# V read back once a pass in four transfers of all 128 rows, and the projected rows' transfers issued behind the products, in a three-layer block on one Trainium2 core

## What is computed

```python
q = jnp.einsum('btc,hdc->bhtd', x, Wq); k = jnp.einsum('btc,hdc->bhtd', x, Wk)
gate_v = jnp.einsum('btc,hec->bthe', x, Ws)
w, sel = jax.lax.top_k(gate_v, K)                       # 2 of 8 experts for each head
mix_v = jnp.einsum('bthk,bthke->bthe', jax.nn.sigmoid(w), one_hot(sel))
proj_v = jnp.einsum('btc,edc->bted', x, Wv)             # 8 experts' projections
v = jnp.einsum('bthe,bted->bhtd', mix_v, proj_v)        # V: 16 heads
attn = softmax(q * scale @ k) @ v
res = jnp.einsum('bthe,bthd,efd->bthf', mask_o, attn, Wo)
```

## Time and profile before

| | us |
|---|---|
| median of 3 runs | 2421.73 |
| lowest and highest run | 2420.21, 2424.61 |
| profiled execution, whole | 2416.01 |
| its span from first to last instruction | 2414.2 |
| PE busy | 2316.1 |
| DVE busy | 2032.5 |
| ACT busy | 2020.9 |
| POOL busy | 1157.8 |

### The profile page before, as it was taken

How to read it: one execution, slowest core, us unless ns; L and a number is a source line. 1 busy time by engine, 2 the same in 40 slices (tenths; PEclk the granted TensorE clock), 3 DMA queues, 4 the chain that set the end, 5 groups by cost and what they waited for, 6 DMA issues and landing times.

```text
span 2414.2 us, 120555 instructions
## 1 busy us (share of the span) xinstructions
PE 2316.1 (96%) x49920; PEld 2149.1 (89%) x49920; DVE 2032.5 (84%) x3626; ACT 2020.9 (84%) x6245; POOL 1157.8 (48%) x1126
## 2 busy tenths in 40 slices
PE   3999999999999999999999999999999999999997
PEld 3988888989899999999989999999999999999987
DVE  5888878888888888888888888888888888888874
ACT  3988787888888888888888888888888888888885
POOL 3454545455354454454454454554554554544431
PEclk9999999999999999999999999999999999999999
DMA  4555455655556556556556556555556555555563
GB/s 125 165 162 155 142 153 146 167 159 166 164 156 178 164 158 177 160 156 175 162 163 173 160 161 172 160 162 162 175 157 168 167 163 163 164 164 163 167 171 105
DMA packets 660701, 388.23 MB, mean 161 GB/s; under 512 B 232512, under 2 KB 585664, under 8 KB 660160
## 3 DMA queue, kind: packets, MB, share of 16 engines
q1 hardware_dynamic: 659728, 379.67, 54.9%
q10 hardware_dynamic: 432, 0.85, 0.1%
HBM read 191.64 MB, written 188.74 MB: 158 GB/s over the span
## 4 chain that ended last, share of the span: by engine, by line
PE 83%; ACT 6%; DVE 6%; issue 3%; POOL 1%; DMA 0%; SPq 0%; DVEq 0%; ACTq 0%; POOLq 0%
PE psT L471 18%; PE psS L426 15%; PE psT L488 7%; PE psS L514 7%; PE psT L439 6%; PE psT L514 6%; PE psT L490 6%; PE psT L489 5%; ACT PB L785 5%; PE psT L483 5%; PE psT L453 4%; DVE NMAX L665 2%; DVE QK L729 1%; PE psT L520 1%; PE psT L572 1%
## 5 line engine op out<-in xcount | busy, mean ns | idle before, releaser
L785 ACT ACTIVATE PB<-psS,NMAX 128x256 f32<-128x256 f32 x2048 | 947.3, 497 | 100.8 <-DVE NMAX L665 99.9
L471 PE MATMUL psT<-V,PT 128*64 128x64 f32 x16384 | 541.3, 224 | 9.9 <-issue 9.4
L471 PEld LDWEIGHTS psT<-V,PT 128*64 128x64 f32 x16384 | 503.2, 138 | 37.8 <-issue 12.4
L785 ACT ACTIVATION_READ_ACCUMULATOR PB<-psS,NMAX 128x1 f32 x2048 | 471.2, 230 | 0.0
L426 PE MATMUL psS<-QK 64*128 64x256 f32 x6144 | 464.0, 290 | 1.2 <-DVE PT L736 1.2
L729 DVE TENSOR_TENSOR QK<-psT,QK 128x512 fp32r<-128x512 f32 x512 | 340.5, 687 | 144.1 <-ACT QK L794 142.2
L426 PEld LDWEIGHTS psS<-QK 64*128 64x128 f32 x6144 | 398.4, 187 | 22.9 <-issue 21.6
L665 DVE TENSOR_REDUCE NMAX<-psS 128x2 f32<-128x512 f32 x512 | 329.0, 684 | 83.5 <-PE psS L426 80.2
L794 ACT ACTIVATE QK<-psT 128x512 fp32r<-128x512 f32 x512 | 299.5, 630 | 84.8 <-PE psT L490 70.7
L891 POOL TENSOR_TENSOR BT<-MT,diagv 128x1024 f32<-128x1024 f32 x128 | 304.9, 2382 | 108.1 <-DMA MT<-MIXd 108.1
L667 DVE TENSOR_REDUCE NMAX<-psS 128x4 f32<-128x1024 f32 x256 | 310.8, 1214 | 0.0
(11 more groups left out here) (120 smaller groups left out, 4776.4 us busy)
## 6 DMA issues: line engine op xcount, KB each, us to landing
Vd<-VM SPq DMA_DIRECT2D x512, 128.0 KB, 2.3
V<-Vd SPq DMA_DIRECT2D x512, 128.0 KB, 3.2
AOd<-AO SPq DMA_DIRECT2D x256, 256.0 KB, 2.5
AR<-AOd SPq DMA_DIRECT2D x256, 256.0 KB, 4.1
PJd<-PJ SPq DMA_DIRECT2D x64, 512.0 KB, 2.8
PR<-PJd SPq DMA_DIRECT2D x256, 128.0 KB, 2.6
MIXd<-MIX SPq DMA_DIRECT2D x64, 128.0 KB, 2.3
MT<-MIXd SPq DMA_DIRECT2D x64, 128.0 KB, 3.2
```

Source lines behind the costliest of these rows:

```text
L471: last = eng.matmul(M[64 * u:64 * u + 64, (t * NT + it) * DH:(t * NT + it + 1) * DH], PT[:, t, jt, cols], V[:, pm % 2, 4 * r + t, jt, :], ...
L785: eng.activation(PB[:, ab, j, it, :], psS[:, ab, j, it, :], ACT.Exp, bias=NMAX[:, ab, j, it:it + 1], accum_out=SUM[:, p % 2, it, 4 * r + t ...
```

## The change

Only SP's program and one waiting number change; all other engines' instructions stay as they are and in their order.

- V is read once a pass, at r = 0 (`load_values(p)`), in four transfers of 128 rows by 512 numbers, 256 KB each, in place of four of 64 rows at r = 3 and four at r = 0, 128 KB each. It waits for both halves' stores.
- At r = 3 SP waits for the product of quarter n - 1 (`wait_full(eng, "product", n - 1)`) ahead of the four reads of PR; behind these stand the four stores of the second half of VM, an AO store and the MIX store.
- The PJ store at r = 2 moves behind the first half's VM stores and the AO store of that quarter.
- The first product of a pass waits for 16 * 4 instead of 32 * 4 steps of `s_value`.

```diff
-            def load_values(q, half):
-                rows = slice(64 * half, 64 * half + 64)
+            def load_values(q):
                 eng.wait_ge(s_split, 4)
-                eng.wait_ge(s_vw[half], 16 * PARTS * (q + 1))
+                for half in range(2):
+                    eng.wait_ge(s_vw[half], 16 * PARTS * (q + 1))
                 wait_full(eng, "product", 4 * (q - 2) + 3)
-                loaded = V[rows, q % 2].rearrange("p h n d -> p (h n d)")
-                stored = Vd[q % 2].rearrange("(p x) -> p x", p=P)[rows]
+                loaded = V[:, q % 2].rearrange("p h n d -> p (h n d)")
+                stored = Vd[q % 2].rearrange("(p x) -> p x", p=P)
...
                 if r == 0 and runs(p):
-                    load_values(p, 1)
+                    load_values(p)
...
-                if r == 2 and runs(p + 2):
-                    q = p + 2
-                    wait_freed(eng, "expert", q, 0)
-                    wait_freed(eng, "expert", q, 1)
-                    if q >= 2:
-                        eng.wait_ge(s_pr, 16 * PARTS * (q - 1))
-                    eng.dma_start(PJd[q % 2].rearrange("(p x) -> p x", p=P),
-                                  PJ[:, :, :, :].rearrange("p e n d -> p (e n d)")).then_inc(s_pjw, 16)
                 if r == 2 and runs(p + 1):
                     store_values(p + 1, 0)
-                if r == 3 and runs(p + 1):
-                    load_values(p + 1, 0)
+                if r == 3:
+                    wait_full(eng, "product", n - 1)
                 if r == 3 and runs(p + 2):
                     q = p + 2
                     eng.wait_ge(s_pjw, 16 * (q + 1))
...
+                if r == 2 and runs(p + 2):
+                    q = p + 2
+                    wait_freed(eng, "expert", q, 0)
+                    wait_freed(eng, "expert", q, 1)
+                    if q >= 2:
+                        eng.wait_ge(s_pr, 16 * PARTS * (q - 1))
+                    eng.dma_start(PJd[q % 2].rearrange("(p x) -> p x", p=P),
+                                  PJ[:, :, :, :].rearrange("p e n d -> p (e n d)")).then_inc(s_pjw, 16)
...
-                    eng.wait_ge(s_value[pm % 2], 32 * PARTS * (pm // 2 + 1))
+                    eng.wait_ge(s_value[pm % 2], 16 * PARTS * (pm // 2 + 1))
```

## The result

| | before | after |
|---|---|---|
| median, us | 2423.17 (4 runs) | 2453.6 (4 runs, 2445.09 to 2467.83) |
| profiled execution, us | 2416.01 | 2452.63 |
| its span, us | 2414.2 | 2450.8 |

The account below looks back on a forecast made before the run. PE, busy 2316.1 of 2414.2 us, was taken as the bound, so only its waits matter. Fetch stalls -5, BT against S +20 and first passes +1 gave +16 on 2421.7: median 2438 us, 8 in 10 range 2409 to 2456.

Parts of the forecast that it names:

- The train: SP's issues at r = 3 from the product's end to V's issue: 6.5 us taken, bounds 5.7 to 7.7.
- V's first issue to MT's landing: Four V issues, then MT landing behind 1 MB, which starts BT: 6.4 us taken, 5.6 to 7.1.
- BT against S: GpSimd's BT starts 0.4 us ahead of DVE's S, blocking it in 20 of 25 odd passes: +20 us.
- BT slips behind S: Rival: BT begins after S in nearly all odd passes and blocking ends: -12, 2409 us; chance 0.14.
- Fetch stalls: PE's 9.4 us of waits inside products, read as lacking instructions, shrink as data leaves the stretch ahead: -5 us.
- costed at nothing: Other readers of SP's later issues, with masks and AR moving 1 to 2.5 us: no cost.
- the change does not free the fetch: Rival: stalls inside products only move; first forecast becomes 2443 instead of 2438; no separate chance given.
- The first passes: First two passes, pipeline still filling and V having less room: +1 us, 0 to 5.
- V's slack: V lands about 3 us ahead of its first product, formerly some 4: costs nothing in the steady part.

## Why the prediction came out as it did

The direction held, and the blocking of DVE by BT was rightly seen. The measured loss was 30 us where 16 were forecast: three terms were off in size, one of them with the wrong sign, and the +20 for BT, twice what came, hid a part of what the fetch cost.

- **The train, 6.5 us from product to V: right.** Measured 6.56 in odd passes and 7.40 in even ones, between the bounds of 5.7 and 7.7. But the two kinds of odd passes kept their distance: 6.9 us in those like 31 and 5.8 in those like 33 (5.7 and 4.6 before), where the working gave both the same 6.5.
- **V's first issue to MT's landing, 6.4 us, 5.6 to 7.1: too short.** It is 7.5 us (median; 6.1 before). MT alone, from its issue, lands in 4.8 us behind 1 MB. I had let the transfers of the AR kind stand as the slow end and taken a value in the middle; the measured one lies past that end.
- **BT against S, +20: mis-sized, +9.** By the two points above BT began 1.5 us behind S in passes like 31 and 0.2 us behind it in those like 33 (medians), not 0.4 us ahead of it in both. I had also counted S alone as exposed and put the cliff at S's start; ST and FW behind it are exposed too, so it stands at FW's start, some 0.5 us later. BT had moved past all three in most passes, so 10 of 25 were hit and not 20. The price of a hit was good: with V read once and nothing else the quarters r = 1 lost 26.4 us on top of the 7.5 that blocking had cost there before, 33.9 us in 24 hit passes or 1.4 each. The rival "BT slips behind S" had its condition met (MT 1.1 us later than taken, against 0.9 asked) and was right for passes like 31; that the blocking then ends altogether was wrong.
- **Fetch stalls, -5: wrong sign, +12.** Of the 27.4 us at line 471, 6.3 are waits for V; 21.1 remain against 9.4. The working named the failing step itself, that V's 1 MB with AR behind it might starve r = 0 and 1, and then took it as a bound of zero. It starved r = 2. The step that failed is "costed at nothing": AR moves by 1 to 2.5 us (measured: 3.1), and since PE hardly waits for AR, that was taken as free. AR's wait is free; its traffic is not: 14.7 us more of waits at the product and 5.0 us more busy time of it in the quarters r = 2, which lost 22 us. The delay of AR was also larger than that of V, because MASKT waits for MASKd behind V's megabyte. The rival "the change does not free the fetch" had the right mechanism and a price of 0 for what measured +12. What was hoped of the change did come, from V once alone: 4.5 us of stalls instead of 9.4.
- **The first passes, +1 (0 to 5): mis-sized, +4.8,** at the upper bound. There are 4.7 us of waits for V in passes 0 and 1, but the kernel before reached pass 0's product only 1.5 us earlier; the lower clock behind the wait gave 1.3 us more, pass 1's wait 1.2. Heads differ by some 2 us from one profiled execution to another (above), so this size is rough.
- **V's slack, about 3 us in the steady part: too generous.** The median left is 1.3 us, with four small waits of 0.3 to 0.5 us (passes 16, 32, 48, 52). The conclusion, nothing to pay, is nearly right.

By what was measured the sum is 9 for BT, 12 for the stalls and 5 for the head, 26 of the 34.5 us between the product starts of the two profiled executions. Most of the remaining 9 us is in PE's busy time: 5.0 us in the broken products of r = 2. The rest is the 1.6 us of small waits for V, 1.2 for the layer norm, 1.4 of stalls at line 483.

The kernel with the product wait but the old place of PJ has more stalls (28.6 us without the waits for V) than the one with both moved (13.7 us), though AR lands at 7.6 and 8.1 us in the two; their times, 1.0116 and 1.0067, have intervals that touch. PJ's place is all that differs. In its old place its 512 KB stand right behind AR and land 10.0 us behind the pass's first product, past the start of the product of r = 2 at 8.6 (without the product wait they land at 8.4); in the kernel with both moved they are issued only at 13.7. So PJ behind a late AR may add to the stalls. That it is the landing that matters isn't tested and stays open.

What is shown: that the blocking of DVE's instructions costs 14 us in the changed kernel; that the stalls are PE at the border of a block of its code; that the product wait carries the rest in r = 2 and that the PJ store alone costs nothing measurable; that a later AR is enough to make such stalls; and that the code packets behind it begin later. What holds them up inside the DMA engines no run shows, and the AO and PJ stores that follow AR may add to it.

## What to carry to other kernels

When a chain of transfers is moved later, follow every transfer in it to what its traffic meets, not only to who waits for its data: here the 1 MB that nobody waited for cost more than the one that was argued over. A collision between two engines has edges on both sides, so count all instructions in a row that can be hit (S, ST and FW), and measure the shift before pricing: half a microsecond decides between free and the full price. And if two edits delay the same thing, try each alone with the collision taken out; here, with BT behind ST in all, reading V once was worth -12 us (0.9943 against 0.9994) and the product wait +42. To tell a want of instructions from other waits, count the engine's instructions up to each wait: a remainder of 256 that returns is the mark.

## What the runs showed of the hardware that was not expected

- Where a transfer lies in time can matter as much as its size: AR 4 us later in each pass (2.2 us behind the first product's start instead of 1.8 ahead) raised the stalls at the product and line 483 from 10.9 to 58.3 us, and the time by some 60 us.
- A transfer behind V's 1 MB landed later by half again than behind its half: MT 4.8 us after issue instead of 3.2, the AO store 3.8 instead of 2.5, while the AR transfers took 4.2 (4.1 before).
- A blocked instruction can be useful: with S freed in the kernel before, 7.5 us were gained in r = 1 and 7.8 lost in r = 3, where stalls rose from 4.9 to 12.7 us.
- Every stall at the product in the two kernels (18 and 32) stands at the same remainder, 193 or 194, of PE's instruction count divided by 256. In pass 32 the two pieces of the broken product take 2.43 us together, where a whole one takes 2.09.
- A DVE instruction of 0.29 us that began 0.23 us behind GpSimd's BT took 2.34 us, until 0.15 us behind BT's end, the same 0.15 us as in the earlier trace rows. One of 0.42 us (FW, two bf16 inputs) took 2.58.
